# Attention: causal mask on the exponentials by GpSimd instead of a mask product, inverse roots on VectorE, a new order of GpSimd's batch

## The reference, cut to what matters

```python
h = _layernorm(x) * (1 + ca) + sa
q, k, v = (einsum('bim,mhd->bhid', h, w) for w in (wq, wk, wv))
q, k = _rope(_rmsnorm(q)), _rope(_rmsnorm(k))
s = einsum('bhid,bhjd->bhij', q * mult, k * mult)      # 256 x 256 per head
s = s - 1e30 * (i < j)                                 # causal
p = softmax(s)
x = x + ga * einsum('bhid,hdm->bim', einsum('bhij,bhjd->bhid', p, v), wo)
h = _layernorm(x) * (1 + cb) + sb
x = x + gb * experts(h)
```

## Time and profile before

| | us |
|---|---|
| median of 3 runs | 1105.14 (1104.69 to 1106.26) |
| profiled execution, first to last instruction | 1104.4 |
| of it attention and routing | about 0 to 800 |
| TensorE busy over the span | 1019.0 |

### The profile page before, as it was taken

The page is one execution under the profiler, slowest core; times in us unless marked ns, Lnnn a source line. Parts: engine busy times, 40 slices in busy tenths (PEclk is TensorE's granted clock), DMA queues, the critical chain, the costliest instruction groups (busy, mean ns, idle before and its releaser), DMA issues. The chain is left out here.

```text
span 1104.4 us, 27346 instructions
## 1 busy us (share of the span) xinstructions
PE 1019.0 (92%) x7434; PEld 791.3 (72%) x7434; DVE 923.8 (84%) x2706; ACT 969.8 (88%) x3517; POOL 825.8 (75%) x1197
## 2 busy tenths in 40 slices
PE   5899999999999999999999999999989999999800
PEld 3478888888888888888888888888865455579600
DVE  4888999989999999888888888888766997778837
ACT  6899999999999999999999999999769999999534
POOL 6665578888888888888878788888745687777744
PEclk9999999999999999999999999999999999999955
DMA  5320000001000000000000000000034233321158
GB/s 150 104 71 14 13 18 23 23 26 34 27 23 26 26 23 14 16 16 16 14 15 16 14 14 16 16 16 16 16 111 129 84 118 104 96 85 40 46 207 261
DMA packets 53704, 57.90 MB, mean 52 GB/s; under 512 B 7964, under 2 KB 42639, under 8 KB 53556
## 3 DMA queue, kind: packets, MB, share of 16 engines
q1 hardware_dynamic: 36468, 35.10, 10.9%
q0 software_dynamic: 8640, 16.87, 4.4%
q10 hardware_dynamic: 8448, 4.20, 1.3%
HBM read 33.08 MB, written 23.97 MB: 52 GB/s over the span
## 5 line engine op out<-in xcount | busy, mean ns | idle before, releaser
L751 ACT ACTIVATE squares<-unit 128x128 f32<-128x128 f32 x1024 | 273.0, 302 | 3.6 <-PE unit L1211 3.4
L563 POOL TENSOR_TENSOR roped<-roped,rope_b 128x512 f32<-128x512 f32 x132 | 174.9, 1326 | 93.8 <-DVE rope_b L1099 91.4
L751 ACT ACTIVATION_READ_ACCUMULATOR squares<-unit 128x1 f32 x1024 | 234.1, 235 | 0.0
L1080 DVE TENSOR_TENSOR roped<-unit,cos_sb 128x512 f32<-128x512 f32 x256 | 174.4, 681 | 31.7 <-ACT squares L751 30.9
L1563 POOL DMA_INDIRECT y_rows<-y_out,place_y x142 | 155.3, 1093 | 54.3 <-issue 40.5
L1099 DVE TENSOR_TENSOR rope_b<-unit,sin_sb 128x512 f32<-128x512 f32 x256 | 174.3, 681 | 0.0
L729 ACT ACTIVATE probs<-scores,rr 128x256 f32<-128x256 f32 x256 | 123.7, 483 | 51.6 <-issue 25.5
L1291 PEld LDWEIGHTS unit<-ident,roped 128*128 128x128 f32 x1024 | 117.9, 142 | 31.9 <-ACT k_t L768 13.1
L1049 DVE SCALAR_TENSOR_TENSOR acc<-pv,den,acc 128x128 f32<-128x128 f32 x448 | 139.0, 341 | 0.3
L1291 PE MATMUL unit<-ident,roped 128*128 128x128 f32 x1024 | 135.2, 275 | 1.7 <-POOL roped L563 1.6
L572 POOL TENSOR_TENSOR roped<-roped,rr 128x1024 f32<-128x1024 f32 x64 | 121.6, 1900 | 9.6 <-DVE roped L1108 8.8
(11 more groups left out here) (310 smaller groups left out, 2972.3 us busy)
## 6 DMA issues: line engine op xcount, KB each, us to landing
shared<-y_rows SPq DMA_DIRECT2D x16, 512.0 KB, 5.6
x_all<-in_L_attn_x SPq DMA_DIRECT2D x32, 128.0 KB, 2.1
h_late<-in_L_ffn_W SPq DMA_DIRECT2D x16, 256.0 KB, 3.5
out_x<-hidden ACTq DMA_DIRECT2D x16, 256.0 KB, 4.4
rope_b<-x_rows SPq DMA_DIRECT2D x13, 258.0 KB, 2.9
tile_x<-x_rows SPq DMA_DIRECT2D x12, 258.0 KB, 3.0
y_rows<-y_out,place_y POOLq DMA_INDIRECT x142, 2.3
ga_b<-mod_dram SPq DMA_DIRECT2D x32, 64.0 KB, 2.9
```

Source lines behind the costliest of these rows:

```text
L563: pool.tensor_tensor(out=roped[parity][:, u, heads], in0=roped[parity][:, u, heads], in1=rope_b[:, u % 2, heads], op=ALU.add)\
L751: nc.scalar.activation(squares[:, c * D:(c + 1) * D], UN[0][:, c * D:(c + 1) * D], ACT.Square, accum_out=ssq[parity][:, u * H + c:u * H + ...
L1080: nc.vector.tensor_tensor(out=roped[parity][:, u, heads].rearrange("p (g c) -> p g c", c=D // 2), in0=UN[0][:, heads].rearrange("p (g c) - ...
```

## The change

The mask product and its constants go. The scores of a head are two products: 128 keys against 256 queries, and 128 keys against 128 queries. Unmasked scores go through the exponential, and GpSimd then sets the entries above the diagonal of the two diagonal blocks to zero in `probs` with one affine_select per head over 128 x (2 x 128) fp32; it waits for the exponentials of the head, and the values' product waits for it (`masked`). GpSimd's `roots`, `newton` and `offsets` become VectorE's `root_sums` at slot (0, 1), `root_step` at (1, 4), (2, 0) and (2, 1), and `offsets` at (2, 2), on 36 columns instead of 40, 8 instructions per iteration for 10 on GpSimd. On ScalarE the guess at h = 1 moves ahead of the copy of `k_t`. On GpSimd the list of an iteration is reordered, with eight masks in it. Six set-up fills of constants, a fill and two selects go.

```diff
-                        nc.tensor.matmul(s[:, P:T], k[:, h, 0:P], q[:, h, P:T], start=True, stop=True)
-                        nc.tensor.matmul(diagonal, ident_bf[:, :], mask, start=True, stop=False)
-                        nc.tensor.matmul(s[:, 0:P], k[:, h, 0:P], q[:, h, 0:P], start=False, stop=False)
-                        nc.tensor.matmul(s[:, T:T + P], k[:, h, P:T], q[:, h, P:T], start=False, stop=True)\
+                        nc.tensor.matmul(s[:, 0:T], k[:, h, 0:P], q[:, h, 0:T], start=True, stop=True)
+                        nc.tensor.matmul(s[:, T:T + P], k[:, h, P:T], q[:, h, P:T], start=True, stop=True)\
                             .then_inc(S["s_done"], 1)
...
-                    wait(pe, "exp_done", 2 * (g + 1))
+                    wait(pe, "masked", g + 1)
                     wait(pe, "acc_done", TT * (g - 1))
...
+                def mask(h):
+                    if C:
+                        g = H * (n - 2) + h
+                        wait(pool, "exp_done", 2 * (g + 1))
+                        blocks = probs[:, h % NPR, :].rearrange("p (a c) -> p a c", c=P)[:, 0:TT + 1:TT, :]
+                        pool.affine_select(out=blocks, in_=blocks, compare_op=ALU.is_ge, fill=0.0, base=0,
+                                           pattern=[[0, TT], [1, P]], channel_multiplier=-1).then_inc(S["masked"], 1)
```

VectorE's new steps:

```diff
+            ROOTS = {(1, 4): 0, (2, 0): 1, (2, 1): 2}
+                def root_sums():
+                    wait(dve, "guess_done", 2 * (n + 1))
+                    wait(dve, "sq_done", cap(NU * H * n, NU * H * NB))
+                    nc.vector.tensor_scalar(vx[:, 0:NLN], ssq[other][:, :], WS * WS * RMS_EPS * D, None, ALU.add)\
...
+                    for k, stats in enumerate((mv[other], mv2[parity])):
...
+                        nc.vector.tensor_scalar(vx[:, NLN + k * TT:NLN + (k + 1) * TT],
+                                                stats[:, :, 1:2].rearrange("p t o -> p (t o)"), LN_EPS, None, ALU.add)\
...
+                def root_step(k):
+                    if k == 0:
+                        wait(dve, "guess_done", 2 * (n + 2))
+                        nc.vector.tensor_tensor(out=correction[:, :], in0=guess[:, :], in1=guess[:, :], op=ALU.mult)\
...
+                    elif k == 1:
...
+                        nc.vector.scalar_tensor_tensor(out=correction[:, :], in0=correction[:, :], scalar=-0.5,
+                                                       in1=vx[:, :], op0=ALU.mult, op1=ALU.mult)\
...
+                    elif k == 2:
+                        wait(dve, "newton_step", 2 * (n + 2))
...
+                        nc.vector.scalar_tensor_tensor(out=rr[other][:, :], in0=correction[:, :], scalar=1.5,
+                                                       in1=guess[:, :], op0=ALU.add, op1=ALU.mult)\
+                            .then_inc(S["rr_done"], 1)
+                def offsets():
+                    wait(dve, "rr_done", n + 2)
+                    for k, stats in enumerate((mv[other], mv2[parity])):
+                        c0 = NLN + k * TT
+                        nc.vector.scalar_tensor_tensor(out=off[other][:, k * TT:(k + 1) * TT],
...
+                            .then_inc(S["off_done"], 1)
...
                 def small(h, slot):
+                    if any(live[1:7]):
+                        if (h, slot) == (0, 1):
+                            root_sums()
+                        elif (h, slot) in ROOTS:
+                            root_step(ROOTS[h, slot])
+                        elif (h, slot) == (2, 2):
+                            offsets()
```

More of the change, by code:

```diff
@@ L508, in body @@
                 other = 1 - parity
[L510 to L557, removed]
                 def add(h):
@@ L597, in body, with low_part, places @@
                 rest = not isinstance(n, int) or 0 <= n - 7 < LAST - 1
[L598 to L616, removed]
+                def mask(h):
[5 more added lines that the diff above has]
+                                           pattern=[[0, TT], [1, P]], channel_multiplier=-1).then_inc(S["masked"], 1)
+                def low_part():
+                    b = n + 1
+                    wait(pool, "hhi_done", b + 1)
+                    wait(pool, "vw_done", TT * (b - 1))
+                    pool.tensor_tensor(out=h_lo[other][:, :], in0=h_t[:, :], in1=h_hi[other][:, :], op=ALU.subtract)\
+                        .then_inc(S["h_ready"], 1)
+                def places():
                     b = n - 6
@@ L622, in body, with scores @@
                                        op=ALU.mult).then_inc(S["place_k_done"], 1)
[L623 to L629, removed]
+                def scores():
                     b = n - 5
@@ L634, in body, with second_weight @@
                                        op=ALU.mult).then_inc(S["scored"], 1)
[L635 to L645, removed]
+                def second_weight():
                     b = n - 6
@@ L659, in body, with choice @@
                                        in1=top_s[:, :, 0:1], op=ALU.subtract).then_inc(S["gapped"], 1)
-                if A:
-                    add(6)
-                if RT:
+                def choice():
                     b = n - 5
@@ L682, in body @@
                         .then_inc(S["rows_tagged"], 1)
+                if n == 0:
+                    for h in range(HH):
+                        add(h)
+                if rest:
+                    scatter(n - 7, other, 1, 0)
+                mask(0)
+                if R:
+                    gated_residual()
+                mask(1)
+                if rest:
+                    scatter(n - 7, other, 1, 1)
+                mask(2)
+                if B:
+                    scale_queries(0)
+                mask(3)
+                if ST:
+                    places()
+                if B:
+                    if A:
+                        wait(pool, "q_added", HH * n + 3)
+                    scale_queries(1)
+                mask(4)
+                if now:
+                    scatter(n - 6, parity, 0, 0)
+                if X:
+                    low_part()
+                if RT:
+                    scores()
+                mask(5)
+                if A:
+                    add(4)
+                if now:
+                    scatter(n - 6, parity, 0, 1)
+                if ST:
+                    second_weight()
+                mask(6)
+                if A:
+                    add(5)
+                if RT:
+                    score_gap()
+                mask(7)
+                if A:
+                    add(6)
+                if RT:
+                    choice()
+                if A:
+                    add(7)
+                if RT:
+                    tag_rows()
             iterations(pool, body)
```

75 lines of the change are left out of this document (32 added, 43 removed).

## The result

| | us |
|---|---|
| before | 1105.70 (1104.69 to 1106.32) |
| after | 1192.02 (1191.80 to 1193.17) |
| ratio | 1.0784, 95% interval 1.0771 to 1.0797 |

The change makes the kernel 7.8% slower. I had forecast slower, by 2%; the range ended at 1148. Part 1 of the page of the kernel after and one of its iterations; the columns are those of the earlier trace rows.

The account below looks back on a forecast made before the run. TensorE's stream was taken as the bound. One iteration's chain summed to 25.49 us against 24.54, taken as +0.9 in 24 iterations (+21.6), plus 1.5 for early ones: 1104.4 + 23 = 1127.5, forecast 1128 us, range 1088 to 1148.

Parts of the forecast that it names:

- TensorE: 0.88 us less an iteration, at most 28 us.: TensorE's scores: each of eight heads loses a 0.11 us mask product, over 32 iterations.
- a rival: All of TensorE's gain arrives, offsets and masks being in time: 1105 - 28 = 1077 us; chance 0.08.
- ScalarE stands for the offsets.: At h = 2 ScalarE's `xn` waits for VectorE's offsets until 424.0, standing 1.5 us each iteration.
- 0.35 (two offsets, with the end of the second and the semaphore): Last term of the count to 424.0 at VectorE's slot (2, 2): both offset steps take 0.35 us.
- The lock: VectorE two-input steps and GpSimd exclude each other, deciding at `mask(0)`: 1143 us, 1148 with root steps held up; chance 0.12.
- The chain: One iteration between starts of h = 0's scores: 7.37, 3.91, 6.34, 2.19, 5.01 and 0.67, together 25.49 us.
- the queue of GpSimd as written: GpSimd's ordered list from `add(4)` to `mask(7)`, 5.01 us, ahead of head 7's product; cited against ScalarE setting the pace.
- Iterations 2 to 6, +0.3 each.: Early iterations without scatters and routing: mainly ScalarE's stand counts, +0.3 us each, 1.5 us in all.
- The masks.: GpSimd's eight added selects on 256 columns: 0.45 us each, bounds 0.29 and 0.73.
- The total stays: GpSimd's work per iteration stays as it was: 3.6 us of masks for 3.3 us of root operations.
- VectorE.: Eight small steps added to VectorE at 0.10 us each, 0.8 us; upper end 0.5 us each.
- Below the period: VectorE's busy time of 21.94 + 0.8 = 22.7 us stays below the iteration's period.

Follow-up runs that it names:

- e4: Kernel before without its mask product, scores of a head in two products, causal mask left out: ratio 0.9903, attention 792.3 us against 802.6.
- e1: Kernel after with GpSimd's queries' scaling waiting for the offsets instead of the inverse roots: ratio 1.0325, attention 834.3 us.
- e7: Kernel after with each two-input offset step written as two one-column steps with one input and a scalar pointer: attention 844.9 us, one run.
- e3: Kernel after without its eight mask selects, causal mask left out: ratio 1.0718, attention 887.1 us.
- e2: Kernel after with the scaling behind the offsets, and all three root steps and the offsets at slot (1, 4): ratio 1.0055, attention 806.5 us.
- e9: e6 with the moved scatter ahead of mask(2) and the first scaling also waiting for VectorE's sum of h = 1: ratio 0.9977, attention 796.4 us.
- e12: e9 with mask(7) ahead of the gap step on GpSimd: ratio 0.9964, attention 796.8 us.
- e8: Kernel before with two score products and the eight masks on GpSimd, roots left on GpSimd: ratio 1.0332, attention 835.0 us.
- e6: Kernel after with scaling behind offsets, root steps and offsets at (1, 2), one scatter moved into the next iteration behind mask(2): ratio 1.0173.

## Why the prediction was wrong

The sign and the place of the first stand were right, the size was not: 86 us where I had 23, and no range of mine held it. Step by step:

- **TensorE: 0.88 us less an iteration, at most 28 us.** As an upper bound it held, but a measured 10.3 us (e4) is what it is worth. I had used the 28 for a rival.
- **ScalarE stands for the offsets.** Right in kind. The term that failed is the last of its sum, "0.35 (two offsets, with the end of the second and the semaphore)". Those steps took 1.89 us, because GpSimd's scaling, released by the same root step, got in first. From the end of the projection of h = 2 to `xn` it was 5.5 us where I had 3.91, and 1.33 us of stand came back to my 1.5 as soon as the order was turned (e1).
- **The lock.** I had the rule and a row for it, worked it out at `mask(0)` alone, put held-up root steps at 5 us in all (1148 for 1143), and gave it 0.12. I did not walk the new VectorE steps past what GpSimd does at the same moment, though both are released by `rr_done`. By the Trainium skill, page SBUF — State Buffer, section SBUF: two separate sides, a two-input step of VectorE and a GpSimd operation that reads SBUF exclude each other for a whole instruction; the traces of after, e1 and e7 agree, the last with the one-input case beside it.
- **The chain.** Its other links came out as summed: 7.51 for 7.37, 6.35 for 6.34, 2.22 for 2.19, 4.98 for 5.01, 0.74 for 0.67, and 27.33 in all with 5.53 for 3.91. Without the lock 25.64 was measured for 25.49. But such links, cut at the same events in each iteration, always add up to the iteration, whatever holds it. And e3 shows that the last ones were not needed for the length: with no masks the iteration was as long. This is a second step that failed: "the queue of GpSimd as written" (`add(4)` to `mask(7)`, 5.01) was not the only way to head 7's product. VectorE's queue, from the cosine product of h = 4 without idle time to the addition of head 5, and 0.15 us from there, takes as long (7.05 + 0.15 for 2.22 + 4.98), and in e1, e2, e9 and e12 it ends last. My sum never asked for that addition, which the product also waits for.
- **Iterations 2 to 6, +0.3 each.** The stand is 2.7 us there too, and iterations 4 to 6 (26.6, 26.1, 26.8) are 3.4, 2.9 and 2.2 us longer than before. The same term.
- **The masks.** 0.41 us for 0.45 in the median, up to 0.92 where a two-input step of VectorE runs beside one. GpSimd's total is 21.01 for 20.41, standing included. "The total stays" held; in e8, where the roots stay, it is 23.2.
- **VectorE.** 0.8 us for eight steps; without the standing offsets it is not much more. Its measured 24.77 us busy contains the time it stood: 24.77 - 21.94 - 1.7 leaves 1.1, and shorter stands are still in that (the first root step takes 0.40 us beside a mask, 0.19 in e3, which has none). "Below the period" was right and not enough: its queue had no idle time where head 7's product waits for it.

## What to carry to other kernels

When one completion releases two engines whose steps shut each other out, as here VectorE's two-input step and GpSimd's scaling, look at who arrives first: the long operation with slack should wait for the short one that others need, even if that adds a wait. A small step moved to a faster engine is priced by what runs beside it, not by its own duration, and a busy engine in a profile may be a standing one: compare an instruction's duration with its usual one. A chain that adds up to the measured time is not yet the chain that holds it: list every wait of its instructions, and take one link out. Before paying for the removal of work from the busiest engine, leave the work out in the kernel as it is, to see what it is worth at most (here 10 of 28 us).

## What I had not expected of the hardware

GpSimd's scatter and scaling can hold VectorE's two-input sum as a pair: 3.05 us when the sum came 0.42 us after a scatter that the scaling followed, 0.69 us when it came 0.17 us after it. It needs no scatter: in e8 the sum came 0.23 us after a select of 0.41 us had started, was not let in between the select and the scaling behind it, and ended 0.56 us after the scaling. So a step that already stands can lose to GpSimd's next operation too. Why a sum 0.17 us after a scatter's start gets through, and one 0.42 us after it does not, these runs don't tell. And the lock can give the same code two iteration times: 24.2 and 26.0 us in e6, with the switch where a piece of other work (the splitting of the expert weights) ended.
